# First layer of a two-layer transformer kernel: row statistics and normalisations spread over steps, head outputs divided by VectorE straight from PSUM, weight differences shared anew between GpSimd and VectorE

## The reference

```
x = x + layernorm(L0_attn(layernorm(x)))     # 32 heads of 16, one shared key/value head, ALiBi, causal
x = x + layernorm(L0_ffn(layernorm(x)))      # block-dequantised 512x512 weight, bias
x = x + layernorm(L1_attn(layernorm(x)))     # 32 heads of 128, 8 key/value heads, RoPE
x = x + layernorm(L1_ffn(layernorm(x)))      # ternary octonion linear, gated
```

```
scores = q_h @ k.T * scale + slope_h * (pos_k - pos_q)    # causal, else -inf
attn   = softmax(scores)                                  # exp(scores - row maximum) / its sum
out_h  = attn @ v                                         # 16 columns
y      = concat(out_h) @ Wo
```

## Time and profile before

| what | value |
|---|---|
| median of 3 runs | 2259.62 us (2256.56 to 2260.6) |
| the profiled execution: its time | 2258.78 us |
| the profiled execution: its span | 2256.8 us, granted clock 0.965 |
| steps 0 to 63 of the first layer | 79.7 to 572.4 us of the span |
| busy share of the span: TensorE, VectorE, ScalarE, GpSimd | 92%, 78%, 62%, 41% |

### The profile page before, as it was taken

How to read it: one execution, slowest core, us unless ns; L and a number is a source line. 1 busy time by engine, 2 the same in 40 slices (tenths; PEclk the granted TensorE clock), 3 DMA queues, 4 the chain that set the end, 5 groups by cost and what they waited for, 6 DMA issues and landing times. The chain is left out here.

```text
span 2256.8 us, 48541 instructions
## 1 busy us (share of the span) xinstructions
PE 2078.5 (92%) x18563; PEld 1258.3 (56%) x18563; DVE 1771.4 (78%) x3711; ACT 1391.5 (62%) x3037; POOL 930.4 (41%) x901
## 2 busy tenths in 40 slices
PE   8688978889767799999999999999999999988998
PEld 3366656566534456666566665656666665533443
DVE  5699898899765787877787887878878787977665
ACT  2555555555644776777777687777777777761222
POOL 0177776678934323233332323333232333353221
PEclk9899989999778999999999999999999999999999
DMA  5210100101022354444444454454344444520100
GB/s 202 78 35 17 44 20 16 46 17 46 3 80 81 71 88 89 90 71 92 85 77 90 81 100 69 81 97 90 68 90 90 71 81 80 101 75 19 38 20 38
DMA packets 390214, 153.81 MB, mean 68 GB/s; under 512 B 358544, under 2 KB 369424, under 8 KB 387936
## 3 DMA queue, kind: packets, MB, share of 16 engines
q1 hardware_dynamic: 389984, 150.71, 30.5%
HBM read 48.69 MB, written 11.53 MB: 27 GB/s over the span
## 5 line engine op out<-in xcount | busy, mean ns | idle before, releaser
L1762 POOL TENSOR_TENSOR q_in_sbuf<-q_in_sbuf,sinq 128x512 f32<-128x512 f32 x128 | 162.6, 1270 | 720.7 <-ACT q_in_sbuf L1894 598.1
L1906 ACT ACTIVATE xp<-xp,nm 128x128 f32<-128x128 f32 (+3 forms) x512 | 281.3, 550 | 199.1 <-DVE nm L1989 199.1
L1788 PE MATMUL bank<-xT_hi,weights_and_hi 128*128 128x512 f16 x1280 | 381.9, 380 | 6.2 <-DVE yacc L2004 3.5
L814 ACT ACTIVATE weights_and_hi<-bank,unit 128x512 f32<-128x512 f32 x320 | 212.0, 687 | 191.4 <-PE bank L612 187.7
L1871 ACT ACTIVATE probs_hi<-xp,rl 128x128 f16<-128x128 f32 (+3 forms) x512 | 245.1, 550 | 67.8 <-DVE rl L2009 64.4
L1958 DVE SCALAR_TENSOR_TENSOR probs_lo<-xp,rl,probs_hi 128x128 f16<-128x128 f32 (+3 forms) x512 | 282.2, 611 | 0.0
L1966 DVE TENSOR_TENSOR q1T_lo<-qf,q1T_hi 128x512 f16<-128x512 f32 x128 | 88.4, 690 | 223.3 <-ACT q1T_hi L1885 223.3
L1989 DVE CUSTOM_DVE_ANT_0 xp<-bank,mask,cs 128x128 f32<-128x128 f32 (+3 forms) x512 | 250.1, 544 | 0.0
L1788 PE MATMUL bank<-xT_lo,weights_and_hi 128*128 128x512 f16 x640 | 243.0, 380 | 0.0
L533 POOL CAST weights_and_hi<-weights_and_hi 128x1024 f16<-128x1024 f32 (+1 forms) x192 | 188.6, 995 | 116.7 <-ACT weights_and_hi L814 116.5
L1788 PE MATMUL bank<-p1T_hi,v_hi 128*128 128x128 f16 x1280 | 223.1, 220 | 3.3 <-DMA p1T_lo<-probs_lo 3.3
(11 more groups left out here) (307 smaller groups left out, 5510.5 us busy)
## 6 DMA issues: line engine op xcount, KB each, us to landing
weights_and_hi<-in_wq SPq DMA_DIRECT2D x8, 1024.0 KB, 5.6
raw_o<-in_wo SPq DMA_DIRECT2D x8, 1024.0 KB, 5.8
x_front<-in_x SPq DMA_DIRECT2D x4, 1024.0 KB, 6.6
q_stack<-q_hi SPq DMA_DIRECT2D x64, 64.0 KB, 2.6
xb<-in_x SPq DMA_DIRECT2D x4, 1024.0 KB, 5.5
wup<-in_wup SPq DMA_DIRECT2D x3, 1024.0 KB, 12.1
fused_scratch<-weights_and_hi SPq DMA_DIRECT2D x12, 256.0 KB, 3.0
x_scratch<-xb SPq DMA_DIRECT2D x3, 1024.0 KB, 4.3
```

The source lines that it names most:

```text
L814: act.activation(px[:, p % 2, i, :], bank_of(("x", p, i))[:, :], ACT.Exp, scale=unit[:, 0:1]).then_inc(s_ed, 1)
L1762: pool.tensor_tensor(qs[:, i % 2, :], qs[:, i % 2, :], rope["sink" if u[0] == "k" else "sinq"][:, :], ALU.mult).then_inc(s_rot, 1)
L1788: ins = pe.matmul(out, lhs(a), rhs(c), start=(first and i == 0), stop=(last and i == 2))
L1906: ins = act.activation(x, x, ACT.Exp, scale=-1.0, bias=nm[:, m % 3, t:t + 1], accum_out=ls[:, m % 3, t:t + 1])
```

## The change

1. `copy_heads`, the buffer `ob` and its semaphore are gone. VectorE takes the reciprocals of the sums from the PSUM bank itself and then, in the same step, multiplies the heads of pair n-8 from the bank (`norm_heads`, now on VectorE). The bank counts as emptied when that is done (`"pv": (s_pf, s_on)`).
2. GpSimd subtracts for blocks 3 and 4 (128x1024 instead of 128x512), VectorE's second difference covers block 2 alone (128x512 instead of 128x1024).
3. The statistics of n1, n2 and n3 are spread over four or two steps (`STATS`), these norms come one or three steps later, ScalarE normalises one tile between two exponentials, over two steps, the additions are spread in the same way, and so are the stacking of keys on ScalarE and the last step of the joined keys on VectorE.

```diff
-        NORM = {"n1": -13, "a1": 30, "n2": 33, "a2": 40, "n3": 43}
+        NORM = {"n1": -10, "a1": 30, "n2": 34, "a2": 40, "n3": 44}
+        STATS = {"n1": (-13, -12, -11, -10), "n2": (33, 33, 34, 34), "n3": (43, 43, 44, 44)}
...
-        signals = {"s": (s_sf, s_sd), "x": (s_ef, s_ed), "pv": (s_pf, s_pd), "m": (s_mf, s_md), "K": (s_kf, s_kd),
+        signals = {"s": (s_sf, s_sd), "x": (s_ef, s_ed), "pv": (s_pf, s_on), "m": (s_mf, s_md), "K": (s_kf, s_kd),
...
                     pool.wait_ge(s_wh, 3 * p + 3)
-                    pool.tensor_tensor(ph[1][:, p % 2, 4, :], px[:, p % 2, 4, :], ph[0][:, p % 2, 4, :],
+                    pool.tensor_tensor(ph[1][:, p % 2, 3:5, :], px[:, p % 2, 3:5, :], ph[0][:, p % 2, 3:5, :],
                                        ALU.subtract).then_inc(s_wc, 1)
...
                 for n in STEPS:
-                    for u in norms_at(n - 3):
-                        if u in add_no:
-                            add_rows(u, (2, 3))
+                    adds_at(n - 4, 3)
+                    adds_at(n - 3, 1)
                     for u in norms_at(n - 1):
                         rstd(norm_no[u])
-                    if 0 <= n - N_LAG < NP:
-                        norm_heads(n - N_LAG)
                     if 0 <= n - X_LAG < NP:
                         weights_hi(n - X_LAG)
-                    for u in norms_at(n - 2):
-                        if u in add_no:
-                            add_rows(u, (0, 1))
+                    adds_at(n - 3, 2)
+                    adds_at(n - 2, 0)
...
-                        if i == 2 and 0 <= n - V_LAG < NP:
-                            copy_heads(n - V_LAG)
...
-                    b = at(n, FRONT["K"] + 1)
-                    if b is not None:
-                        stack_keys(b)
-                    for u in norms_at(n - 1):
-                        normalise(u)
+                        for u in norms_at(n - 2) if i < 2 else norms_at(n - 1) if i > 2 else ():
+                            normalise(u, i + 2 if i < 2 else i - 3)
+                        if i > 2 and at(n, FRONT["K"] + 1) is not None:
+                            stack_keys(at(n, FRONT["K"] + 1), 0, i - 3)
+                        if i < 2 and at(n, FRONT["K"] + 2) is not None:
+                            stack_keys(at(n, FRONT["K"] + 2), 1, i)
...
                 def weights_lo(p, i):
-                    c = slice(2 * i, 2 * i + 2)
+                    c = slice(2 * i, 2 + i)
...
+                def norm_heads(p):
+                    b, c = p // PAIRS, 2 * (p % PAIRS) * E0
+                    if p % GP == 0 and b >= 1:
+                        dve.wait_ge(*filled[("o", b - 1, p % PAIRS // GP)])
+                    dve.wait_ge(s_ro, p + 1)
+                    o = pv_out(p)
+                    dve.tensor_tensor(on[:, :, c:c + 2 * E0].rearrange("p t (e c) -> p e t c", e=2),
+                                      o[:, :, :, 0:E0], ro[:, p % 2, :, :].unsqueeze(3).to_broadcast([P, 2, TT, E0]),
+                                      ALU.mult).then_inc(s_on, 1)
...
                         maximise(n, (2, 3))
+                    if 0 <= n - V_LAG < NP:
+                        sum_reciprocals(n - V_LAG)
                     for u in extra[:1]:
                         evacuate(u)
+                    if at(n, FRONT["K"] + 1) is not None:
+                        add_key_maxima(at(n, FRONT["K"] + 1))
+                    some_statistics(stats_at(n)[:1])
+                    if 0 <= n - V_LAG < NP:
+                        norm_heads(n - V_LAG)
                     if 0 <= n < NP:
                         maximise(n, (4,))
...
                     for u in extra[1:]:
                         evacuate(u)
+                    some_statistics(stats_at(n)[1:])
```

More of the change, by code:

```diff
@@ L226, in layer0 @@
         GP = 4
-        X_LAG, V_LAG, N_LAG = 6, 8, 9
+        X_LAG, V_LAG = 6, 8
         GQ, GKV, GO, GF = range(4)
@@ L407, in norms_at, with stats_at @@
             return out
+        def stats_at(n):
+            return [(kind, b, t) for kind in STATS for t in range(TT)
+                    for b in (at(n, STATS[kind][t]),) if b is not None and has(kind, b)]
         norms = [u for n in STEPS for u in norms_at(n)]
@@ L829, in maxima_hi, with stack_keys @@
                                    scale=-1.0 / MAXU).then_inc(s_mh, 1)
[L831 to L838 removed]
+                def stack_keys(b, i, e):
+                    k, half = (kz, ks)[i], ("even", "odd")[e]
+                    act.wait_ge(s_kb, 2 * b + i + 1)
+                    if b >= 2:
+                        act.wait_ge(*filled[("x", PAIRS * (b - 1) - 1, 4)])
+                    act.activation(k[:, b % 2, e, :], kb[:, i, :], ACT.Copy,
+                                   scale=row[half][:, 0:1]).then_inc(s_kr, 1)
                 for n in STEPS:
@@ L1003, in maxima_lo, with pv_out, some_statistics @@
                                              mh[0][:, g % 2, :], ALU.mult, ALU.subtract).then_inc(s_md, 1)
+                def pv_out(p):
+                    return bank_of(("pv", p))[:, 0:2 * TT * EV].rearrange("p (e t c) -> p e t c", e=2, c=EV)
                 def sum_reciprocals(p):
-                    dve.wait_ge(*emptied[("pv", p)])
-                    if p >= 3:
-                        dve.wait_ge(s_on, p - 2)
-                    dve.reciprocal(ro[:, p % 3, :, :], ob[:, p % 3, :, :, E0]).then_inc(s_ro, 1)
+                    dve.wait_ge(*filled[("pv", p)])
+                    dve.reciprocal(ro[:, p % 2, :, :], pv_out(p)[:, :, :, E0]).then_inc(s_ro, 1)
+                def norm_heads(p):
[7 more added lines that the diff above has]
+                                      ALU.mult).then_inc(s_on, 1)
+                def some_statistics(tiles):
+                    for kind, b, t in tiles:
+                        if kind == "n1":
+                            dve.wait_ge(s_xf, 16 * b)
+                            statistics(t, xf)
+                        else:
+                            dve.wait_ge(s_ad, TT * add_no["a" + str(int(kind[1]) - 1), b] + t + 1)
+                            statistics(t, xb)
                 scalars()
```

58 lines of the change are left out of this document (12 added, 46 removed).

## The result

| | before | changed |
|---|---|---|
| median of the runs | 2259.66 us (2256.56 to 2260.6, 4 runs) | 2306.58 us (2305.64 to 2308.16, 4 runs) |
| span of the profiled execution | 2256.8 us | 2306.2 us |

The account below looks back on a forecast made before the run. VectorE was taken to set the pace of most first-layer steps, TensorE that of steps with long products. Terms -34 + 13 + 32 + 13 - 12 = +12 us gave 2271 us, whole range 2237 to 2290.

Parts of the forecast that it names:

- (d): VectorE beside GpSimd's wider difference of 2.2 us: more waiting for the shared SBUF way, 32 us more, 0.5 per step.
- (e): Weighed-values bank emptied later: in 13 places VectorE finds its last maximum not ready, 1.0 us each, 13 us more.
- (a): VectorE's second difference half as wide: 64 x 0.53 = 34 us less.
- steps of 6.4 to 6.6 us: Sign of being right: plain steps, the 14 lasting up to 6.35 us, would take 6.4 to 6.6 us.
- (b): Heads multiplied on VectorE from PSUM, 64 instructions at 0.20 us: 13 us more.
- (c): Copies leave ScalarE, 17.7 us, nothing gained; GpSimd loses the heads and its 1024-wide difference should take 2.2 us.
- (f): Side work dealt out over steps: a quarter of VectorE's 47.8 us idle time won, 12 us less.
- The second layer and the ends are untouched: Outside the first layer's steps: no change, so no term in the sum.
- The first rival: GpSimd's long difference finds room where VectorE does not need the shared way: 2241 us, chance 0.33.
- the cancelling one: Waiting grows by 0.3 us per step, late bank and dealing out equal: within 4 us of 2259.6, chance 0.15.
- GpSimd becomes the bound: GpSimd falls behind, ScalarE's fourth exponential waits for its difference, each of 13 places costs 2 us: 2295 us, chance 0.08.

Follow-up runs that it names:

- drop3: only3 with block 3's difference left out altogether, zeros standing in for it: 2220.0 us, ratio 0.9825 to the kernel before.
- only3: Kernel before with only the side work dealt out (part 3) and the early instruction; heads and blocks as before: 2234.7 us, ratio 0.9895.
- early instruction: One-column GpSimd tensor_tensor that nobody reads, added during the loads at the start; added to the changed kernel it measured 2300.9 us against 2306.6.
- no1: Changed kernel with the early instruction, but heads copied by ScalarE and multiplied by GpSimd as before: 2263.8 us, ratio 1.0021 to the kernel before.
- lib: Changed kernel, all three parts, plus the early instruction: 2300.9 us, ratio 1.0187 to the kernel before.
- only2: Kernel before with nothing but part 2, GpSimd subtracting blocks 3 and 4: 2286.3 us, ratio 1.0129.
- split: no1 with GpSimd's difference of two blocks issued as two instructions of one block: 2252.4 us, ratio 0.9968 to the kernel before.
- act_lumps: only3 with ScalarE normalising its four tiles and stacking the keys in a lump behind its five exponentials: 2249.7 us, ratio 0.9955 to the kernel before.
- reduce_no1: no1 with VectorE's copy of the maxima and addition of epsilon written as reductions: 2266.0 us, ratio 1.0027 to the kernel before.
- reduce_3: only3 with VectorE's copy of the maxima and addition of epsilon written as reductions: 2232.4 us, ratio 0.9874 to the kernel before.

## Why the prediction was wrong

The direction was right, and the two mechanisms that (d) and (e) name are in the traces. The sizes failed, first of all in step (a), "64 x 0.53 = 34 us less", and then in (e), "13 x 1.0 = 13 us more".

- **(a) failed.** VectorE's differences did become 34.4 us shorter in drop3 (145.0 against only3's 179.4), but the kernel only 14.7. I had counted VectorE's work as the path. My own rows said otherwise: the long steps, where VectorE idles at times anyway, were given a low price for added waiting in (d) and the full price for saved work in (a).
- **(d) was right for the differences**, +34.5 measured and +32 forecast, but left out the copy of the maxima, the addition of epsilon and the joining of the keys, +16.3, which wait in the same way. To these 50.8 us stand 43.8 of time. Together (a) and (d) are +29 and not -2: 31 of the 36 us by which the forecast was short. Its form was wrong too: steps of 6.4 to 6.6 us were to show it, and of the 14 plain steps nine last 5.2 to 6.35 us, six of them under 6.0, while four of the other five have taken on statistics.
- **(e) was right in place and mechanism and too small by more than half.** The eleven places in steps 0 to 62 cost 26 to 28 us and not 11. The 1.07 us was read in step 40, where TensorE had the full clock; behind the wait for the heads in step 24 it had half, and in the eleven places together the clock falls by 0.08 to 0.13. The waits before the last maximum grew by 14.6 us (22.5 against 7.9), and the low parts of the transposed tiles, which hang on the same bank, wait 8 us more.
- **(b)**, 13 us, is right as VectorE's time, and of it little arrives: 2 to 4 us in the 52 steps outside the places, as with (a). Together (b) and (e) were forecast at 26, and part 1 measures 30 to 40, by what stands beside it. That this sum is nearer than its terms is luck.
- **(c)** held: GpSimd did not become the bound, and ScalarE never waits for its difference in the changed kernel.
- **(f)**, 12 us, was undersized for the dealing out alone (24), and near what it gives beside both other parts (15). That it is worth less there is open.
- **"The second layer and the ends are untouched"** does not cover what a later first norm does on GpSimd: 6 to 7 us of loading. They fall into step 7, inside the steps that the sum counts, and no term has them.

From one kernel to the next the whole account is: part 3 with the early instruction -24 (only3), part 2 +29 (no1), part 1 +37 (lib), the early instruction gone again +6 (changed): +48, where the sum had -12, -2, +26 and nothing, +12. The misses are -12, +31, +11 and +6; with another order of the parts they shift by up to 10.

The first rival and the cancelling one needed the waiting to grow by 0.3 us per step or less; it grew by 0.8 (50.8 over 64 steps). "GpSimd becomes the bound" came nearest in time, 2295, but not by its cause; only its price of 2 us per place was nearer than the forecast's.

## What to carry to other kernels

Work taken off the busiest engine and work put on it have different prices where the bound changes from step to step: here 14.7 us of time for 34.4 saved, and 43.8 for 50.8 of added waiting. A wait of TensorE is priced too low if the clock behind it is taken as the full one: read it in a row where TensorE has just waited as long. Where two engines take turns on a shared way, add up everything that must pass it on both sides, small copies included, and try a long instruction in two (11.4 us gained with two blocks, nothing with one); a wait moved off one instruction is paid by the next. Before an instruction of a kind that an engine has not yet run is moved, look where its first use stands and what hides it.

## What the runs showed that I had not expected

- A copy of 128x8 elements from SBUF to SBUF on VectorE takes 965 to 1256 ns in the mean beside GpSimd's two-block differences (lib, no1, only2) and 574 to 751 beside one-block ones (split, drop3, before, act_lumps); as a reduction over one element it takes 170 ns in either (reduce_no1, reduce_3).
- TensorE's granted clock in the eleven places falls from 0.93 to 0.85 when part 1 alone is made, and in the other steps not at all.
- GpSimd's first two-operand instruction after the start runs 7.0 us behind its MODIFY_POOL_CONFIG (66.8 to 73.8, 111.3 to 118.2).
- GpSimd's casts, which have one input, became longer as well: 1275 ns in the mean in the changed kernel, 1104 before.
- Two GpSimd instructions of one block take 2 x 1506 ns beside this VectorE, one of two blocks 2379.
